# Cross-attention on one core: scores in two products instead of three, with the queries' parts moved by six DMAs per unit

## What is computed

```python
q = split_heads(x @ Wq)                # 32 x 20 x 256 x 16
k = split_heads(ctx @ Wk)              # 32 x 20 x 77 x 16
v = split_heads(ctx @ Wv)
p = softmax(einsum('bhsd,bhld->bhsl', q, k) / sqrt(16))
x = merge_heads(einsum('bhsl,bhld->bhsd', p, v)) @ Wo + bias + x
```

## Time and profile before

| | before |
|---|---|
| median of 3 runs | 929.22 us (926.53 to 930.88) |
| profiled execution, first to last instruction | 926.1 us |
| TensorE matmul busy | 903.4 us, 11518 instructions |
| TensorE weight loads busy | 681.3 us |
| VectorE busy | 685.7 us |
| ScalarE busy | 544.6 us |
| GpSimd busy | 402.8 us |
| DMA | 112.41 MB, mean 121 GB/s |
| granted TensorE clock | 0.997 |

### The profile page before, as it was taken

The page is one execution under the profiler, slowest core; times in us unless marked ns, Lnnn a source line. Parts: engine busy times, 40 slices in busy tenths (PEclk is TensorE's granted clock), DMA queues, the critical chain, the costliest instruction groups (busy, mean ns, idle before and its releaser), DMA issues.

```text
span 926.1 us, 28090 instructions
## 1 busy us (share of the span) xinstructions
PE 903.4 (98%) x11518; PEld 681.3 (74%) x11518; DVE 685.7 (74%) x1221; ACT 544.6 (59%) x549; POOL 402.8 (43%) x229
## 2 busy tenths in 40 slices
PE   8899999999999999999999999999999999999897
PEld 5777778777787777777777777777778777777665
DVE  3775787868778686787868688786786868678557
ACT  4456565656556556666556656556665656656553
POOL 3424263633436263366624446364344625433224
PEclk9999999999999999999999999999999999999999
DMA  6313534445444544545555444544534544443342
GB/s 203 102 32 80 138 93 132 135 124 148 98 119 119 164 131 110 149 115 140 141 148 140 102 118 113 137 132 123 134 95 118 139 131 134 102 130 78 86 134 94
DMA packets 80526, 112.41 MB, mean 121 GB/s; under 512 B 21200, under 2 KB 37878, under 8 KB 80400
## 3 DMA queue, kind: packets, MB, share of 16 engines
q1 hardware_dynamic: 80208, 110.35, 44.4%
q10 hardware_dynamic: 192, 0.26, 0.2%
HBM read 60.24 MB, written 22.24 MB: 89 GB/s over the span
## 4 chain that ended last, share of the span: by engine, by line
PE 82%; DVE 6%; DMA 4%; SPq 3%; issue 2%; ACT 1%; POOL 1%; DVEq 0%; ACTq 0%; POOLq 0%
PE pR L307 27%; PE pR L444 14%; PE pA L391 10%; PE pR L378 8%; PE pR L287 4%; PE pR L329 4%; PE pR L257 4%; DMA X<-in_xT 2%; PE pA L397 2%; PE pR L261 2%; DVE OS L1090 2%; SPq L1434 1%; PE pA L307 1%; DVE QL L995 1%; PE pR L244 1%
## 5 line engine op out<-in xcount | busy, mean ns | idle before, releaser
L763 ACT ACTIVATE P<-pA 77x2048 f32<-77x2048 f32 x160 | 300.4, 1878 | 197.2 <-PE pA L397 196.9
L1034 DVE TENSOR_REDUCE Mx<-pR 128x4 f32<-128x308 f32 (+1 forms) x480 | 259.2, 575 | 31.8 <-PE pR L378 26.6
L1293 POOL TENSOR_TENSOR On<-On,OS 128x1024 f32<-128x1024 f32 (+1 forms) x58 | 105.8, 1845 | 257.8 <-DMA OS<-rd 257.8
L307 PE MATMUL pR<-OS,Wo 128*128 128x512 f32 x638 | 168.1, 402 | 2.9 <-DVE OS L1090 2.1
L444 PE MATMUL pR<-P,VA 77*17 77x256 f32 x2480 | 157.4, 385 | 0.8 <-ACT P L763 0.5
L378 PEld LDWEIGHTS pR<-KH,QH 32*128 32x128 f32 x1280 | 96.3, 183 | 70.8 <-issue 46.6
L391 PE MATMUL pA<-QH,KH 32*77 32x256 f32 x1280 | 145.0, 291 | 0.1
L1258 POOL TENSOR_TENSOR XS<-X,XS 128x1024 fp32r<-128x1024 f32 x31 | 74.0, 2387 | 152.1 <-ACT XS L649 152.1
L378 PE MATMUL pR<-KH,QH 32*128 32x154 f32 x1280 | 131.5, 283 | 7.8 <-DVE X L1101 2.2
L307 PEld LDWEIGHTS pR<-OS,Wo 128*128 128x128 f32 x638 | 113.8, 188 | 33.2 <-issue 6.3
L391 PE MATMUL pA<-QL,KH 32*77 32x256 f32 x1280 | 134.9, 275 | 0.0
(11 more groups left out here) (161 smaller groups left out, 1289.6 us busy)
## 6 DMA issues: line engine op xcount, KB each, us to landing
On<-Oraw SPq DMA_DIRECT2D x244, 64.0 KB, 2.7
OS<-rd SPq DMA_DIRECT2D x58, 256.0 KB
C<-in_cT SPq DMA_DIRECT2D x16, 616.0 KB, 7.9
X<-in_xT SPq DMA_DIRECT2D x16, 512.0 KB
y<-X SPq DMA_DIRECT2D x16, 512.0 KB, 4.0
X<-y SPq DMA_DIRECT2D x16, 512.0 KB
out<-X SPq DMA_DIRECT2D x15, 512.0 KB, 4.0
X<-in_xT SPq DMA_DIRECT2D x16, 256.0 KB
```

Of the source, the lines that this page charges most:

```text
L307: f = pe.matmul(p[:, :], W[:, k, c0:c0 + 128], S[:, s, :], start=(i == 0), stop=(i == len(pairs) - 1))
L763: act.activation(P[0:L, i % PR, :, :], pA[0:L, :, :], ACT.Exp, scale=float(D) ** -0.5).then_inc(p_done, 1)
L1034: dve.tensor_reduce(Mx[:, :, :].rearrange("p t (j i) -> p j t i", j=4)[:, j:j + banks, :, i:i + 2], pR[:, bank:bank + banks, 0:2 * LK].rea ...
L1293: pool.tensor_tensor(On[rows, blocks, :], On[rows, blocks, :], recips(u, part).bitcast(F32), ALU.mult).then_inc(o_mul, 1)
```

## The change

Within 32 partitions the two heads now alternate: head p of a pair has the even (p = 0) or the odd partitions (p = 1). The columns of Wq and Wk and the rows of Wo are permuted for it on the host. A key tile for head p has hi on its own rows and zeros on the other's. `keys` puts, by DMA, the rounded keys onto the free rows of KL, so that a KL tile holds lo on its own rows and hi on the others. `queries_a` and `queries_b` put the queries' lo beside their hi in the same way: for even heads in QH itself (its odd rows are overwritten by QL's even rows, once the maxima products of the unit have read QH), for odd heads in a new single buffer TB. Then KL x (hi, lo) gives lo x hi + hi x lo in one product, and keys_by_tokens has two products for three; a run has eight steps for ten. QL and TB have one buffer each. PV now writes 32 columns per head (the head's values in every other row), so that `natural` is 4 DMAs; `spread` has 5, `sums` of the last block 2.

```diff
 def keys_by_tokens(i, j):
-    h = i // 3
-    Q_ = (QH, QL, QH)[i % 3]
+    h = i // 2
+    q = QH[32 * j:32 * j + 32, u % 2, c0:c0 + SQ] if pp == 0 else TB[32 * j:32 * j + 32, c0:c0 + SQ]
-        kt = (KH, KH, KL)[i % 3][32 * j:32 * j + 32, ms, u % 4, h, :]
+        kt = (KH, KL)[i % 2][32 * j:32 * j + 32, ms, u // 2 % 2, pp, u % 2, h, 0:L]
...
-for step in range(10):
+for step in range(8):
...
-    if n is not None and step == 8:
+    if n is not None and step == 6:
         take_pair(second, 1)
...
-        pe.wait_ge(q_lo[ms], u + 1)
-        pe.wait_ge(k_lo[ms], u // 2 + 1)
+        pe.wait_ge(d_tb[ms // 2], 32 * (u + 1))
+        pe.wait_ge(d_k[ms // 2], 32 * (u // 2 + 1))
...
-    f = pe.matmul(bank[32 * j:32 * j + D + 1, ...], VA[0:L, u % 2, b, h:C + H:H], src,
+    f = pe.matmul(bank[32 * j:32 * j + 32, ...], values_and_one(u, b, h), src,
...
 def Q_lo(u, m):
     dve.wait_ge(q_hi[m][u % 2], u // 2 + 1)
+    if u:
+        dve.wait_ge(d_tb[m // 2], 32 * u)
...
+def keys(w, tail):
+    for m in ((0, 1), (2,))[tail]:
+        sp.wait_ge(k_lo[m], w + 1)
+    for p in range(2):
+        sp.dma_start(lo[there].bitcast(F32), hi[here].bitcast(F32)).then_inc(d_k[tail], 16)
+def queries_b(u, tail):
+    cols = (slice(0, 2 * N), QCOLS[2])[tail]
+    for m in ms:
+        sp.wait_ge(q_hi[m][u % 2], u // 2 + 1)
+    if u:
+        sp.wait_ge(s_pe, NG * (u - 1) + (4, 5)[tail])
+    sp.dma_start(TB[ODD, cols].bitcast(F32), QH[ODD, u % 2, cols].bitcast(F32)).then_inc(d_ta[tail], 16)
+    for m in ms:
+        sp.wait_ge(q_lo[m], u + 1)
+    sp.dma_start(TB[EVEN, cols].bitcast(F32), QL[ODD, cols].bitcast(F32)).then_inc(d_tb[tail], 16)
+def queries_a(u, tail):
+    sp.wait_ge(x_pe, 2 * (NG * u + (4, 5)[tail]))
+    sp.wait_ge(d_ta[tail], 16 * (u + 1))
+    sp.dma_start(QH[ODD, u % 2, cols].bitcast(F32), QL[EVEN, cols].bitcast(F32)).then_inc(d_tb[tail], 16)
...
-    for m in ((0, 1), (2,))[part]:
-        sp.dma_start(recips(u, part)[:, m % 2, :].bitcast(F32),
-                     src.broadcast_to([MT[m] // D, D, N])).then_inc((d_rb, d_rbt)[part], 16)
+    for m in range(2):
+        for p in range(2):
+            sp.dma_start(recips(u, part)[(EVEN, ODD)[p], m, :].bitcast(F32),
+                         src[m].broadcast_to([4, D, N])).then_inc(d_rb, 16)
...
 # SP, even unit
     put_recips(v, 1)
+    keys(w, 0)
     spread(v, 0)
     spread(v, 1)
     store(z)
     load_c(u // 2 + 2)
-    sums(u, 0)
+    queries_b(n, 0)
     load_x(u + 3)
+    queries_a(n, 0)
+    queries_b(n, 1)
+    keys(w, 1)
+    queries_a(n, 1)
 # SP, odd unit
     sums(v, 2)
+    sums(v, 0)
     sums(v, 1)
...
     values(u + 1)
+    queries_b(n, 0)
     spread(v, 0)
     spread(v, 1)
+    queries_a(n, 0)
     store(z)
     sums(u, 0)
+    queries_b(n, 1)
+    queries_a(n, 1)
```

More of the change, by code:

```diff
@@ L22 @@
 L4 = L * 4
+LP = L + 1
 MT = [128, 128, 64]
@@ L30 @@
 QC = 2 * N + SQ
+OSLOT = (0, 2, 1, 3, 4)
+HH = H // 2
+HPOS = [HH * (1 - h % 2) + h // 2 for h in range(16)] + [18, 19, 8, 9]
 WORDER = ["Wk0", "Wq0", "Wv0", "Wo0", "Wk1", "Wv1", "Wq1", "Wo1"]
@@ L138, in build @@
         d_va = [sem(f"d_va{i}") for i in range(2)]
+        d_k = [sem(f"d_k{i}") for i in range(2)]
+        d_ta = [sem(f"d_ta{i}") for i in range(2)]
+        d_tb = [sem(f"d_tb{i}") for i in range(2)]
         d_zg, d_rw, d_rb = (sem(f"d_{n}") for n in ("zg", "rw", "rb"))
@@ L471, in PV_last @@
                                 first = half == 0
-                            f = pe.matmul(dst, VL[0:L, b, h:2 * C:H] if what == "OL" else ones[:, pp, :], src,
+                            g, vl = HPOS[h], VL[0:L, b, :]
+                            if what == "ZL":
+                                lhs = stripes[:, pp:pp + 32] if m < 2 else blocks[:, D * pp:D * pp + 32]
+                            else:
+                                lhs = columns(vl, g, H)
+                            f = pe.matmul(dst, lhs, src,
                                           start=first, stop=True, skip_group_check=True)
@@ L1116, in _ @@
             maxima(0, 0, 0, 1, 2)
+            Q_lo(0, 0)
             K_hi(0, 2)
@@ L1144, in _ @@
                         maxima(n, 1, 1, 0, 2)
+                        Q_lo(1, 2)
                         K_lo(0, 2)
@@ L1147, in _ @@
                     elif u < NU - 2:
+                        Q_lo(u + 1, 2)
                         K_hi(w, 0)
@@ L1400, in values @@
                         if u < NU - 1:
-                            src, dst = VS[row:row + rows, t, :], VA[done:done + rows, half, b, 0:C]
+                            src, dst = VS[row:row + rows, t, :], VA[done:done + rows, half, b, HH:HH + C]
                         else:
@@ L1405, in values @@
                         done += rows
-            def sums(u, m):
+            def keys(w, tail):
+                if w >= NW:
+                    return
+                for m in ((0, 1), (2,))[tail]:
+                    sp.wait_ge(k_lo[m], w + 1)
+                for p in range(2):
+                    here, there = (EVEN, ODD) if p == 0 else (ODD, EVEN)
+                    if tail:
+                        lo, hi = (t[:, w % 2, p, :, :].rearrange("q s k -> q (s k)") for t in (KL2, KH2))
+                    else:
+                        lo, hi = (t[:, :, w % 2, p, :, :, :].rearrange("q m s b k -> q m (s b k)") for t in (KL, KH))
+                    sp.dma_start(lo[there].bitcast(F32), hi[here].bitcast(F32)).then_inc(d_k[tail], 16)
@@ L1498, in _ @@
             weight_load("Wo", 0)
+            keys(0, 0)
             values(0)
+            queries_b(0, 0)
+            queries_a(0, 0)
+            queries_b(0, 1)
+            queries_a(0, 1)
             for u in range(NU):
-                v, z = u - 1, u - 2
+                n, v, z, w = u + 1, u - 1, u - 2, u // 2 + 1
                 if u % 2 == 0:
```

189 lines of the change are left out of this document (105 added, 84 removed).

## The result

The changed kernel takes **1282.4 us** in the median of 4 runs (1278.59 to 1285.72), where the kernel before takes 930.05 (926.53 to 932.15) beside it: a ratio of 1.3775 [1.3721, 1.3829], 38% slower. The forecast was 1165 us with a range of 980 to 1200: the direction and the chain of waits came, the size did not.

A forecast was written before the change was run, and what follows sets the result against it. TensorE was taken as the bound, its matmuls busy 98% of 926.1 us. Stalls and slow clock of 273 us less 37.5 gained gave 1161.6, plus 3.1 to the runs' median: 1165 us, range 980 to 1200.

The forecast's parts named there:

- The chain: Even unit: store's landing holds load_x, then queries_a, then VectorE's Q_lo, so TensorE stands in run(u,4) for bank 2.
- The stall of 14.6 us: Even unit, run(u,4): TensorE wants bank 2 at 446.4 but Q_lo ends at 461.0; bounds 3.1 and 17 us.
- the sum: 14 x (14.6 + 1.7 + 3.2) = 273, less 37.5, gives +235.5 us on the profiled execution's 926.1.
- the clock's 1.7 us per pair of units: TensorE's clock falls after the even unit's stall, costing 1.7 us of work once per even unit (0 to 3).
- the gain of 37.5 us: Two of ten steps fewer in each of 160 runs, 0.235 us per run, 37.5 us on TensorE's path.
- the odd unit's stall of 3.2 us: Odd unit: max_rows waits for Q_lo, held by queries_a behind the spread; 3.2 us, between 0 and 4.5.
- Pairs: The stalls and clock loss were counted for 14 even units with store and spread, of 16 pairs of units.
- The spread: Outermost count 4, estimated at 98 GB/s: 2.7 us later before load_x in even units, also slower ahead of odd queries_a.
- The PV loads: PV's weight loads of 32 columns for 17 cost nothing, as each load lies beside the matmuls.
- A: Rival: queries_a isn't held by the load ahead, or the spread isn't slowed: 1044 us, with neither effect 982; chance 0.22.
- B: Rival: everything lands at its least, even stall 3.1 us, no clock loss: 935 us; chance 0.09 above 0.5% slower.
- C: Rival: the wait is covered, store and queries_a landing before TensorE needs bank 2: 892 us; chance 0.04.

The follow-up runs named there:

- e5: The changed kernel without the queries' DMAs, their waits and the queries' lo parts in the scores, and with a spread source of outermost count 16: 935.8 us.
- e4: The changed kernel with reciprocals of blocks 0 and 1 written four times, so the spread's source has outermost count 16 instead of 4: 1156.6 us.
- e1: The kernel before with lo keys x hi queries left out of the scores, runs of eight steps for ten, nothing else changed: 919.5 us.
- e2: The changed kernel without the queries' six DMAs per unit, the waits for them and the queries' lo parts in the scores: 1013.6 us.
- e3: The changed kernel with load_x(u+3) of even units moved behind all DMAs of the queries on SyncE's queue: 1226.1 us.
- e9: The changed kernel with only SyncE's order changed: the DMAs of the queries' blocks 0 and 1 come before the spread: 1284.7 us.
- e14: e12 with queries_b issued by ScalarE around S(u,3) and S(u,4), and queries_a alone on SyncE: 999.0 us.
- e12: The changed kernel with spread of outermost count 16, QL's block 0 double, and SyncE's order placing queries_a before load_x (even), queries_b after spread (odd): 1121.4 us.

## Why the forecast was wrong

**The chain was right.** Which instruction waits first, what stands behind it and where TensorE stops came as forecast. In the even unit shown the forecast, in times from run(u,3)'s end, had TensorE wanting bank 2 at +3.8, load_x issued at +7.6 and queries_a landed at +17.7; the trace has +4.0, +8.0 and +17.9. The stall of 14.6 us was 14.7 here, and 13.9 in the mean of the fifteen (209.1 / 15). That the landing agrees to 0.2 us is in part luck. Its 0.6 us for a write to be known, like the 1.2 us of receipt in the odd unit, stands on no row, and no run shows either. And one link was misplaced, nearly without harm: TB<-QH was taken to land early, but it took 10 us behind the spread, keys and load_c, and held queries_a until 1.3 us after load_x was issued.

**The failed step is the sum**, in three of its terms: the clock's 1.7 us per pair of units, the gain of 37.5 us with all other edits at nothing, and the odd unit's stall of 3.2 us. The runs show 4.8 us per pair for the clock, +5 us in place of the 37.5 gained, and 5.0 us for the odd stall.

| us | forecast | measured |
|---|---|---|
| TensorE's stalls on Q_lo, even and odd | 14 x (14.6 + 3.2) = 249 | 209.1 + 75.3 = 284 |
| slow clock | 14 x 1.7 = 24 | 964.7 - 892.6 = 72 |
| gain and the edits at nothing | -37.5 | +5 (e5) |
| sum | +235.5 | +362, against +352 measured |

The 10 us too many are waits of e5 that the stalls took the place of: by the idle times the stalls add 275 us and not 284.

- *Pairs.* TensorE stalls in 15 pairs, not 14: 18 us.
- *The odd stall.* 5.0 us in the mean for 3.2, 27 us in all. queries_a was issued 5.2 us after queries_b and landed 7.8 us later, 13.1 for the forecast's 11.0. Counting its data beside the spread's receipt explains 0.5 of these 2.1 us; the rest is a later issue (5.2 for 4.35) and a slower landing behind the spread. e4 shows that the spread's shape is the cause: with it changed 9.7 of the 75.3 us are left.
- *The clock.* This is the largest miss, 48 us. The earlier trace rows show dips after idle times of 1 us, and the price was taken from them. After an idle time of 15 us all of the next 4 us ran at 1.2 GHz, and the odd unit paid as well, where nothing was put down: 4.8 us per pair for 1.7.
- *The gain.* 10 to 20 us for 37.5 (e1), 18 by the steps. A step's distance was multiplied by the steps removed, while the second pair of maxima came only 0.11 us sooner per run. The remaining edits give back 16 us (by the spans) to 25 (by the distances) with the fast spread, e5 against e1. 4 us of it are matmul time and the rest idle time; how it divides over the 32-column PV, the keys' copies and the four writes of e5 was not tried.
- *The spread.* It was costed only by what it adds ahead of the queries' copies. e2 against e5 shows that it costs 69 us with no query copy behind it. This isn't one more term for the table above: in the kernel after its price lies in the stalls, and e4 takes 135 us off there.

**The PV loads** were rightly costed at nothing so far as TensorE's matmuls show: 16 matmuls of a PV take 1.10 us at 607.58 for 1.07, and all of them together 160.3 us for 157.4. A load of 32 columns takes 142 ns, in the kernel after and in e5 alike, for the 113 of the earlier trace rows. The Trainium skill ("TensorE: Matmul & The Clock Gate", LDWEIGHTS) has the load grow with its columns, and it did, but by 29 ns for 15 columns where the forecast's estimate from the page was 12.5; the 2480 loads' rise would be 72 us if nothing covered it, and the matmuls show 3 of them.

**The rivals.** A (982 to 1044) left out one or both of the two effects, queue order and slow spread; e3 and e4 show both at work. B and C needed a short landing: the copies do land in 2.3 us when no load, spread or store is ahead of them (e9), and even then the time is 1285, because the spread pays. So C, the gain with the wait covered, was further off than its landing times said. Part of the chances on A should have gone above 1200: the range's upper end was set by the stall alone, the clock's own bound of 3 us was below the 4.8 measured, and the gain had none.

**On the queue.** The Trainium skill ("DMA: Bandwidth & Descriptors", Queues, rings and completion order) has descriptors consumed in ring order on each DMA engine; 7.9 us behind the load against 2.3 without it (e3) agree. The same page (Why a DMA increments its semaphore by 16 and not by 1, on how many engines) has a copy use the largest number of engines up to 16 that divides its outermost counts; the tail's 13% share of 16 engines and e4's 135 us agree. It also says (Issuing engines are not separate DMA queues) that issuing from several engines saves only the issue time, usually small. Here e14 against e12 saves 117 us with the same copies. That is more than the issue time of 4 DMAs of 0.6 us per unit, an estimate of 77 us in 32 units at most. The likely reason is that the waits no longer stand in one program, but this is not shown apart from the second queue; for the bandwidth no run here says otherwise.

## What to carry to other kernels

A DMA that waits for another's landing on an in-order queue is paid by everything behind it; before adding one, write down for each later DMA of that queue who needs it when, because moving the waiting one forward only changed who paid (e9). Try a broadcast source with an outermost count of 16, even at the price of writing it several times: it was worth 69 to 135 us here. And price a stall of TensorE with its slow clock after it, and a shortened loop by a run of it, not by the steps alone.

## What was not expected of the hardware

- A 256 KB copy within SBUF landed in 2.3 us in the median with no load, spread or store ahead of it (e9), in 7.9 behind them (queries_a in the kernel after), and once in 10.0 (TB<-QH at 605.89).
- Broadcasting the reciprocals from DRAM (640 KB per unit) with an outermost count of 4, in 4 DMAs for blocks 0 and 1, and not of 16, in 2, cost 69 us in the kernel without the queries' copies, and 135 with them.
- After 14.7 us without a matmul TensorE's granted clock was 0.50 in the next 4 us, 3.66 of them busy. It stood at 1.00 in 610 to 612, when the idle time had begun at 609.65, at 0.58 in 612 to 614 and at 0.50 from there on. Over the whole kernel that is 72 us of 352.
- Less idle time of TensorE did not mean a faster clock: e9 has 63 us less of it than the kernel after, and 64 us more matmul time.
